# A graph network on one core: the first phase picks the rows of 3 of its 32 tiles per step out of SBUF by one-hot products instead of gathering them

## The reference, cut to what matters

```python
x = silu(edge_radial @ W1 + b1)
x = silu(x @ W2 + b2)
tpw = x @ W3 + b3                      # 256 weights per edge
hs_e, hv_e = h[src, :8], h[src, 8:]    # rows of the source nodes
m0 = ALPHA * (einsum(hs_e * sh0, W00) + INV_SQRT3 * einsum(hv_e, sh1, W110))
m1 = ALPHA * (einsum(hs_e, sh1, W01) + einsum(hv_e * sh0, W10))
agg = segment_sum(concat([m0, m1]), dst)
```

## Time and profile before

| | us |
|---|---|
| median of three runs | 13643.32 |
| the three runs | 13603.05, 13643.77, 13643.32 |
| profiled execution, its time | 13606.3 |
| its span, first to last instruction | 13604.4 |
| busy PE, DVE, POOL, ACT over the span | 12726.5, 10671.1, 10087.9, 7810.4 |
| last gather of the first phase issued at | 3982.9 |

### The profile page before, as it was taken

How to read it: one execution, slowest core, us unless ns; L and a number is a source line. 1 busy time by engine, 2 the same in 40 slices (tenths; PEclk the granted TensorE clock), 3 DMA queues, 4 the chain that set the end, 5 groups by cost and what they waited for, 6 DMA issues and landing times.

```text
span 13604.4 us, 240038 instructions
## 1 busy us (share of the span) xinstructions
PE 12726.5 (94%) x75547; PEld 9594.3 (71%) x75547; DVE 10671.1 (78%) x17694; ACT 7810.4 (57%) x14096; POOL 10087.9 (74%) x10542
## 2 busy tenths in 40 slices
PE   7888888888879999999998999999998999999997
PEld 3444444444448888888886888888886888888886
DVE  7888878888887777777777777777776777777777
ACT  1222222222227777777775777777775777777775
POOL 7777777777767777777776777777776777777775
PEclk9999999999989999999998999999998999999998
DMA  2111111111111111111111111111111111111111
GB/s 52 21 23 21 22 21 21 22 21 22 21 37 33 34 34 34 34 34 33 34 33 43 34 34 33 34 34 34 34 34 40 34 34 34 34 34 33 33 34 43
DMA packets 941460, 434.99 MB, mean 32 GB/s; under 512 B 681631, under 2 KB 894076, under 8 KB 941120
## 3 DMA queue, kind: packets, MB, share of 16 engines
q0 software_dynamic: 339456, 186.75, 9.1%
q1 hardware_dynamic: 431032, 217.76, 6.0%
q10 hardware_dynamic: 170888, 29.48, 1.2%
HBM read 396.32 MB, written 36.84 MB: 32 GB/s over the span
## 4 chain that ended last, share of the span: by engine, by line
POOL 43%; PE 35%; issue 15%; DVE 4%; DMA 2%; SPq 1%; POOLq 0%; ACT 0%; DVEq 0%; ACTq 0%
POOL xg L618 43%; PE ps L1791 18%; PE ps L1774 7%; PE ps L1684 3%; PE ps L1806 2%; PE ps L1701 1%; DVE big L1247 1%; PE ps L1666 1%; DMA big<-in_rad 1%; PE ps L1794 1%; PE ps L1638 1%; DMA xg<-in_x,idx 1%; PE ps L1672 1%; DVE big L1245 0%; PE ps L1757 0%
## 5 line engine op out<-in xcount | busy, mean ns | idle before, releaser
L618 POOL DMA_INDIRECT xg<-x_rows,idx x7329 | 6989.0, 954 | 2309.7 <-issue 2229.5
L1791 PE MATMUL ps<-x_high,row_hot 128*128 128x512 f32 x12276 | 4984.4, 406 | 35.7 <-DVE big L1444 15.8
L1791 PE MATMUL ps<-x_low,row_hot 128*128 128x512 f32 x12276 | 4797.0, 391 | 0.0
L867 ACT ACTIVATE row_hot<-row_of,window_ids 128x256 fp32r<-128x256 f32 (+1 forms) x8232 | 3194.9, 469 | 1290.4 <-PE ps L1794 1290.4
L618 POOL DMA_INDIRECT xg<-in_x,idx x3125 | 3009.2, 963 | 974.2 <-issue 940.2
L1791 PEld LDWEIGHTS ps<-x_high,row_hot 128*128 128x128 f32 x12276 | 2310.9, 188 | 705.6 <-issue 253.4
L1444 DVE TENSOR_TENSOR big<-ps,col_hot 128x512 f32<-128x512 f32 x2058 | 1413.9, 687 | 1592.7 <-PE ps L1794 837.1
L1791 PEld LDWEIGHTS ps<-x_low,row_hot 128*128 128x128 f32 x12276 | 2313.3, 188 | 418.3
L1774 PE MATMUL ps<-big 128*128 128x128 f32 x18816 | 2397.6, 281 | 10.9 <-DVE big L1456 10.8
L1774 PEld LDWEIGHTS ps<-big 128*128 128x128 f32 x18816 | 2203.2, 193 | 12.8 <-DVE big L1456 12.8
L872 ACT ACTIVATE row_hot<-row_hot 128x1792 fp32r<-128x1792 f32 (+1 forms) x1176 | 1777.4, 1511 | 90.3
(11 more groups left out here) (162 smaller groups left out, 10055.0 us busy)
## 6 DMA issues: line engine op xcount, KB each, us to landing
row_of<-pick_rows SPq DMA_DIRECT2D x294, 448.0 KB
xg<-x_rows,idx POOLq DMA_INDIRECT x7329, 2.4
xg<-in_x,idx POOLq DMA_INDIRECT x3125, 2.4
carry<-carry_items SPq DMA_DIRECT2D x392, 48.0 KB
agg_rows<-rts ACTq DMA_DIRECT2D x294, 64.0 KB
meta<-in_coord_t SPq DMA_DIRECT2D x294, 48.0 KB
big<-in_rad SPq DMA_DIRECT2D x196, 64.0 KB
idx<-in_src_t SPq DMA_DIRECT2D x392, 16.0 KB
```

Source lines behind the costliest of these rows:

```text
L618: return nc.gpsimd.indirect_dma_start(out=dst_tile, out_offset=None, in_=table, in_offset=bass.IndirectOffsetOnAxis(ap=index, axis=0))
L867: far = nc.scalar.activation(hot[:, :, b, :], row_of[:, par, ks.start:ks.stop, :], ACT.Abs, bias=window_ids[:, b:b + 1], scale=-1.0)
L1791: nc.tensor.matmul(ps[:, bank, :], row_hot[:, half, at, b, :], x_part[:, b * ROW:b * ROW + ROW], start=(b == 0 and n == 0), stop=False)
```

## The change

1. From step 19 on the first phase gathers 29 tiles. Tiles 15, 23 and 31 (`FIRST_PICKS`) are picked from the input's table in SBUF: ACT forms their `row_hot` between its silus, PE runs `first_pick` (14 matmuls, the same code as in the layers, into bank 4) after the item sums of e = 1, 3 and 5, and DVE selects (`first_select`) after the sums of e = 3, 5 and 7. The rows go into `xg` of the next step.
2. The third layer works on two row tiles: the hidden values of the two tiles stay in partitions 0 to 63 and 64 to 127, one activation writes both, and products with 64 rows each go to `tile_position` 0 and 64 and to two banks. The bias comes from a product of ones with `b3_parts` (float32r, 512 columns) per bank. The radial numbers are laid out for that, which takes four DMAs for a half instead of one.
3. The item sums use one bank (`SUMS = 1`) instead of two; that frees bank 4. `sum_inputs(e-1)` stands right behind the products of e. DVE's products of the first column are joined for four tiles.
4. In SP's program the radial numbers come ahead of the carry row. PE takes `l0_degrees` and, at e = 7, the item sums ahead of the third layer. Semaphore counts follow.

The core of the diff:

```diff
-TPW = (2, 3, 5, 6)
-SUMS = (1, 4)
+TPW = (2, 5)
+SUMS = 1
+FIRST_PICK = 4
+FIRST_PICKS = slice(2, 7, 2)
...
+        FORM_FROM = 2 + 2 * WB + 2
...
 # SP, load_radials
-                sp.dma_start(rad[0:2 * MUL, half], radials_of(...)).then_inc(rad_loaded[half], 16)
+                for h, j in FOUR:
+                    sp.dma_start(radials_to(half, h, j), radials_of(..., h, j)).then_inc(rad_loaded[half], 16)
...
 # ACT, second_layer and l0_step
-                for h in range(2):
-                    own = slice(HID * h, HID * h + HID)
-                    two = nc.scalar.activation(h2_s[0:HID, f % 2, h, :], ps[own, 0, :], ACT.Silu, bias=b2[own, 0:1])
-                two.then_inc(h2_act[f % 2], 1)
+                nc.scalar.activation(h2_s[:, f % 2, :], ps[:, 0, :], ACT.Silu, bias=b2[:, 0:1]).then_inc(h2_act[f % 2], 1)
...
+                    if rest and f == 0:
+                        if due(n):
+                            act.wait_ge(first_pick_done, FP * n)
+                        far(one, coming, range(WB)).then_inc(first_form, 1)
+                    if rest and f == 1:
+                        act.wait_ge(first_form, 2 * n + 2)
+                        near(one, FP - FIRST_PAIR)
+                    if ahead and f == 2:
+                        act.wait_ge(first_row_loaded[par], 8 * (twice - FORM_FROM))
+                        if not isinstance(n, int) or n >= 0:
+                            act.wait_ge(first_pick_done, FP * n + FIRST_PAIR)
+                        far(two, after, range(cut))
+                    if ahead and f == 3:
+                        far(two, after, range(cut, WB)).then_inc(first_form, 1)
+                        act.wait_ge(first_form, 2 * n + 3)
+                        near(two, FIRST_PAIR)
...
 # DVE, l0_step
+                        v.tensor_tensor(pr[:, :, :, 0], tpw[:, :, 0], four[:, :, :, 0]..., ALU.mult)
+                        for h in range(2):
+                            made = v.tensor_tensor(pr[:, h, :, 1:4], tpw[:, h, 1]..., four[:, h, :, 1:4]..., ALU.mult)
+                        made.then_inc(prod_ready[e % 4], 1)
+                        if e:
+                            sum_inputs(i, e - 1)
+                        if picks and e in (3, 5, 7):
+                            first_select(i, par, (e - 3) // 2)
...
 # PE, third_layer
+                for h in range(2):
+                    nc.tensor.matmul(both[:, h], ones_r[rows[h], :], b3_parts[rows[h]], start=True, stop=False,
+                                     tile_position=(HID * h, 0))
+                for j in range(2):
+                    at = P * (2 * (e % 2) + j)
+                    for h in range(2):
+                        tr = nc.tensor.matmul(both[:, h, :, j, :], h2_s[rows[h], f % 2, at:at + P],
+                                              w3[rows[h], :].rearrange("p (t x) -> p t x", t=2), start=False,
+                                              stop=(j == 1), tile_position=(HID * h, 0))
...
 # PE, l0_step
+                for e in range(8):
+                    f = e // 2
+                    if e == 0 and due(i):
+                        l0_turn(i - 1)
+                    if e % 2 == 0 and f + 2 < groups:
+                        second_layer(i, f + 2)
+                    if e % 2 and f < 3 and f + 3 < groups:
+                        first_layer(i, f + 3)
+                    if e == 7:
+                        if due(i):
+                            pe.wait_ge(R_ready, i)
+                        l0_degrees(i)
+                    pe.wait_ge(prod_ready[e % 4], 2 * i + e // 4 + 1)
+                    if e == 7:
+                        item_sums(e)
+                    if f + 1 < groups:
+                        third_layer(i, e + 2)
+                    if e < 7:
+                        item_sums(e)
+                    if picks and e in (1, 3, 5):
+                        first_pick(i, e // 2)
+                if groups == 7:
+                    first_layer(i, 6)
```

More of the change, by code:

```diff
@@ L344, in steps_of, with rows_in @@
             return (path.steps + 1 - par) // 2
-        def rows_in(path, par, q, phase, twice):
+        def rows_in(path, par, q, phase, twice, late=False):
             if phase < 0:
                 return 0
+            whole = 2 * steps_of(path, par)
+            if phase == 0 and path.picks:
+                left = QUART - sum(QUART * q <= s < QUART * q + QUART for s in first_tiles)
+                unpicked = FORM_FROM + 2 * (1 - par)
+                if isinstance(twice, int):
+                    got = 8 * QUART * min(twice, unpicked) + 8 * left * max(twice - unpicked, 0)
+                    padding = (sum(s >= last_tiles(path) and s not in first_tiles
+                                   for s in range(QUART * q, QUART * q + QUART))
+                               if twice == whole and (path.steps - 1) % 2 == par else 0)
+                    return got - 16 * padding
+                return 8 * left * twice + 8 * (QUART - left) * unpicked if late else 8 * QUART * twice
             mine = [QUART * q + r for r in range(QUART) if not (phase and QUART * q + r in path.picks)]
-            whole = 2 * steps_of(path, par)
             earlier = rows_in(path, par, q, phase - 1, whole)
@@ L562, in load_picks @@
                         sp.wait_ge(row_hot_ready, used)
+                    else:
+                        sp.wait_ge(first_row_hot, FORMED)
                     sp.sem_inc(loads_go, 1)
@@ L775, in goes_row, with far, near, l0_step @@
                                ).then_inc(goes_ready, 1)
-            def l0_step(i, groups):
+            def far(to, rows, blocks):
+                for b in blocks:
+                    ins = nc.scalar.activation(to[:, :, b, :], rows, ACT.Abs, bias=window_ids[:, b:b + 1], scale=-1.0)
+                return ins
+            def near(to, n):
+                to = to.rearrange("p k b e -> p (k b e)")
+                nc.scalar.activation(to, to.bitcast(F32), ACT.Relu, bias=1.0, scale=-1.0).then_inc(first_row_hot, n)
+            def l0_step(i, groups, par=0, twice=0, rest=False, ahead=False):
+                two, one = row_hot[:, 0, 0:FIRST_PAIR], row_hot[:, 1, 0:FP - FIRST_PAIR]
+                coming = row_of[:, 1 - par, FIRST_PAIR:FP, :]
+                after = row_of[:, par, 0:FIRST_PAIR, :]
+                n, cut = i - FORM_FROM, (WB + 1) // 2
                 for f in range(4):
@@ new lines, in third_layer, with pick_product @@
+                tr.then_inc(tpw_ready[e % 4], 1)
+            def pick_product(bank, hot, padding=False):
+                for b in range(0 if padding else WB - 1):
+                    for n, x_part in enumerate((x_high, x_low)):
+                        nc.tensor.matmul(ps[:, bank, :], hot[:, b, :], x_part[:, b * ROW:b * ROW + ROW],
+                                         start=(b == 0 and n == 0), stop=False)
+                for n, x_part in enumerate((x_high, x_low)):
+                    tr = nc.tensor.matmul(ps[:, bank, 0:TAIL * CH], hot[:, WB - 1, :],
+                                          x_part[:, FULL_F:FULL_F + TAIL * CH],
+                                          start=(padding and n == 0), stop=(n == 1))
+                return tr
```

307 lines of the change are left out of this document (188 added, 119 removed).

## The result

The changed kernel takes **13702.02 us**, the median of six runs (13699.78 to 13705.4); the kernel before has 13643.7 in the same sitting. The ratio is 1.0047, with a 95% interval from 1.0034 to 1.0060: slower by 0.3 to 0.6%. The forecast was 13700, from 13500 to 13870.

What follows compares the result with a forecast made beforehand. POOL's gathers bound the first phase (40.4 us a step); after the change a loop through PE, DVE and ACT would, at 41.1. 0.7 us more over 79 steps is 55 us; 57 was added to 13643.3: 13700 us, range 13500 to 13870.

Steps and rivals of the forecast that it cites:

- POOL no longer sets the pace: First phase, steps with picks: POOL, at 36.6 us a step, runs ahead until it waits for features.
- 29 x 1.2625 = 36.6 us: First-phase step if POOL's gathers kept setting the pace: 36.6 us, kernel 2.2% less; not taken as the forecast.
- The third layer, 1.3 us: PE's third layer of four tiles on two row tiles: 1.3 us, against 1.82 before.
- the column strips of the earlier trace: PE's item sums: four strips, each of 512 columns, take 0.99 us together, so strips run side by side.
- the upper bound of 2.4: Third layer if row tiles run one after the other: 2.4 us, 520 us more (14220); chance 0.07.
- the walk: One first-phase step followed through the four engines' written orders, 0.2 us per hand-over: 41.1 us a step.
- The closed loop of 41.1 us: First-phase step through PE, DVE, PE and ACT: 9.4, 8.5, 15.9, 6.3 and 1.0 us, against 40.4 before.
- three waits that it named: Per step: DVE about 3 us for item sums of e = 2; PE 1 for ACT, 1.8 for products of e = 4.
- Half a microsecond of trust in the walk: Accuracy claimed for the step, since over the old orders it gave DVE waits near those in the trace.
- 55 us over 79 steps: First phase, steps 18 to 96: 0.7 us more per step, 55 us in all.
- The faster rival: First-phase overlap better than walked, step under 39.9 us, floor DVE's 37.4; gain at most 237 us (13406); chance 0.2.
- DVE's 37.4 us: DVE's sum of work for one first-phase step with three selections, without one wait: 37.4 us.

Runs made afterwards that it cites:

- fourth kernel: The changed kernel without picks and with the three tiles not gathered either from step 19 on: 13360.47 us, ratio 0.979 to the kernel before.
- seventh kernel: The changed kernel without the third layer's bias products, 16 products of 512 columns a step less: 13635.22 us, ratio 1.0008 to the kernel before.

## Why the prediction was right, point by point

- **POOL no longer sets the pace.** Right: 5.0 us of waits for features a step. The gathers' worth, 29 x 1.2625 = 36.6 us, was 36.95 when nothing else was in the way (fourth kernel).
- **The third layer, 1.3 us.** Right, 1.30. The choice by the nearest row, the column strips of the earlier trace rows, and the charge of 0.10 for a change of tiling and 0.10 for the first load hold. Taken apart they fit too, as a sum: without the bias it is 1.06 (0.86 + 0.10 + 0.10), and the bias costs 0.24 (0.23). Only the expectation of the seventh kernel, which took 0.34 for the bias from the trace of the changed one, was off. At the upper bound of 2.4 the walk would have given 14220.
- **The closed loop of 41.1 us.** Right in size, 41.24 measured, and in kind. The step from 2008.47 to 2050.00 in the trace can be cut at the walk's joints: PE 16.39 us to ACT's silu at 2024.86, 6.51 to PE's product at 2031.37, 9.76 to DVE's reduction at 2041.13, 8.87 to PE at 2050.00, together 41.53, where the walk has 15.9, 6.3, 9.4 and 8.5 and 1.0 for the hand-overs. And moving four ACT instructions gives 36 us, moving DVE's scan 114 us, both together what they give alone, and no work was taken away. Of the three waits that it named, the one for item sums was 2.7 to 2.9 us (3 foretold), PE's for the products of e = 4 1.3 to 1.6 (1.8), PE's for ACT 0.4 (1.0).
- **What the walk had wrong** is the last of these waits. DVE loses 0.7 us at the head of each step, waiting for its own last selection before the features; the walk had no such wait. It delays the turn and DVE's products of e = 0, for which PE waits 1.0 us, a wait that the prediction does not name, and so PE's wait for ACT shrinks from 1.0 to 0.4. The sum runs through ACT's leg and has neither wait as a term, so it was not touched; the error shows only where the loop is opened: the walk gave the ACT move 79 us (36 measured) and both moves together 232 (158 by the steps).
- **Half a microsecond of trust in the walk** was about right for the kernel itself (0.1 off), and too much for its variants, which were off by up to 0.9 us, and by 2.0 where the clock fell (40.65 against 42.7). The walk ran at full clock throughout; I had said that short waits might lower it. In the changed kernel they do not (1.00), with the third pick gone they do.
- **The end of the first phase, and the time.** 55 us over 79 steps were forecast; 79 x 0.79 is 62, and 67 came. (The prediction adds 57 to the median where its sum has 55, a slip of 2 us.) That the whole time came within 2 us of the forecast is luck: six executions of the kernel before lie between 13603 and 13650. The layers did not move beyond what executions differ by, and the new form of the step without picks costs 6 us in the phase.
- **The faster rival** had a ceiling that nothing here contradicts (a step cannot go under DVE's 37.4 us; the shortest with three picks is 38.32) and the right cause (waits that could be hidden), but not in the order as written: two moves and an earlier selection get to 38.32.

## What to carry to other kernels

When work is taken from the engine that sets the pace and spread over the others, their sums of work are only a floor; walk one period through all written orders and look for the chain that comes back to itself, and then ask which instruction in it could stand elsewhere. Here the change lost 0.5% as written and gains 1.2% with the same instructions, three groups of them in other places. Price a smaller version of a change too, but look at the clock in it: here two picks were slower than three, because without the third PE stood still for 2.1 us in its place, and the clock fell.

## What the runs showed of the hardware that was not expected

- With two picks, all 24 waits of 2.1 us on PE for DVE's products in 1000 us brought the clock to 1.2 GHz behind them (item sums 1.54 and 1.74 us in place of 0.89 and 1.0), where the changed kernel, with waits of 1.3 to 1.6 us and more work, kept 2.4 GHz throughout. In the kernel without bias products 7 of 13 waits of 1.83 to 1.88 us did. 3 us of idle products a step repaired it and made the kernel faster by 0.4% (ratios 1.0060 and 1.0103).
- The length of the wait did not decide it alone: 12 waits of 2.2 us at the same place had the low clock behind them with two picks, and none of the 12 had once PE ran the idle products.
- Two row tiles of 64 rows with float32 operands take 0.96 us for four products of 256 columns, beside 1.73 us on the whole array (the 1.82 of the earlier trace rows less the change of tiling): the full factor of two, less 0.1 us. Their order in the program matters by 0.1 us.
